# Four graph layers on one core: where TensorE's in-order list holds the probabilities-times-values step

## The reference, cut to what matters

```python
x = _layernorm(x + _L0_gnn_ref(x, adj, adj, L0_gnn_b), axis=-1)
x = _layernorm(x + _L1_gnn_ref(x, L1_gnn_W, L1_gnn_a, L1_gnn_beta, adj), axis=-1)
x = _layernorm(x + _L2_gnn_ref(x, adj, L2_gnn_weight, L2_gnn_bias), axis=-1)
x = _layernorm(x + _L3_gnn_ref(x, adj, L3_gnn_Wq, L3_gnn_bq, L3_gnn_Wk, L3_gnn_bk, L3_gnn_Wv, L3_gnn_bv), axis=-1)
```

## Time and profile before

| what | value |
|---|---|
| device time, median of 3 runs | 2768.54 us (2766.62 to 2768.99) |
| device time of the profiled execution | 2768.19 us |
| its span, first to last instruction | 2766.4 us |
| TensorE busy | 2696.7 us, 97% |
| VectorE, ScalarE, GpSimd busy | 69%, 53%, 54% |
| mean granted TensorE clock | 0.989 |

### The profile page before, as it was taken

One profiled execution on the slowest core, in us unless ns is written; L12 is line 12 of the kernel. 1 busy time (PEld: TensorE's weight loads), 2 busy tenths in 40 slices (PEclk: granted clock), 3 DMA queues, 4 the chain that ended last, 5 costly groups with the idle time before them and its releaser, 6 DMA issues.

```text
span 2766.4 us, 60531 instructions
## 1 busy us (share of the span) xinstructions
PE 2696.7 (97%) x19593; PEld 2383.7 (86%) x19593; DVE 1904.6 (69%) x6165; ACT 1470.6 (53%) x4360; POOL 1480.9 (54%) x1806
## 2 busy tenths in 40 slices
PE   4899999999999999999999999999999999999996
PEld 3788888888888888888888888888888888888886
DVE  7766766676676676776677767667667667667753
ACT  3355555555555555555555555555555555555544
POOL 5555555555555555555555555555555555555541
PEclk7999999999999999999999999999999999999998
DMA  3000000000000000000000000001000000000000
GB/s 123 16 20 28 27 23 27 27 23 27 27 23 27 20 30 27 19 31 27 19 27 31 20 27 31 19 27 31 20 27 30 20 27 29 21 27 27 13 16 24
DMA packets 41607, 75.19 MB, mean 27 GB/s; under 512 B 5584, under 2 KB 5712, under 8 KB 41424
## 3 DMA queue, kind: packets, MB, share of 16 engines
q1 hardware_dynamic: 41424, 73.49, 8.2%
HBM read 39.92 MB, written 33.55 MB: 27 GB/s over the span
## 4 chain that ended last, share of the span: by engine, by line
PE 96%; DVE 1%; issue 1%; ACT 1%; DMA 0%; SPq 0%; POOL 0%; ACTq 0%; POOLq 0%; DVEq 0%
PE rot L796 23%; PE rot L798 23%; PE rot L797 22%; PE score L944 5%; PE rot L904 5%; PE rot L896 5%; PE rot L853 4%; PE rot L952 3%; PE rot L926 2%; PE rot L873 2%; PE rot L877 2%; PE s_bank L861 1%; PE att_bank L932 0%; DVE x L644 0%; DVE att_e L659 0%
## 5 line engine op out<-in xcount | busy, mean ns | idle before, releaser
L360 POOL TENSOR_TENSOR x2b<-x,bias 128x512 f32<-128x512 f32 x128 | 207.6, 1621 | 495.3 <-DVE x L644 495.3
L338 POOL TENSOR_TENSOR ve<-mv,eps_col 128x1 f32<-128x1 f32 (+1 forms) x448 | 89.5, 200 | 666.5 <-ACT e L503 348.4
L796 PE MATMUL rot<-w_hi,y_hi 128*128 128x512 f32 x1024 | 426.3, 416 | 5.2 <-DVE y_lo L634 4.3
L798 PE MATMUL rot<-w_hi,y_lo 128*128 128x512 f32 x1024 | 404.2, 395 | 0.0
L797 PE MATMUL rot<-w_lo,y_hi 128*128 128x512 f32 x1024 | 402.9, 393 | 0.0
L549 ACT ACTIVATE probs<-score,sc_nmax 128x128 f32<-128x128 f32 x1024 | 358.9, 379 | 11.0 <-DVE sc_nmax L757 10.9
L634 DVE TENSOR_TENSOR y_lo<-rot,y_hi 128x512 fp32r<-128x512 f32 x128 | 88.5, 692 | 375.6 <-ACT y_hi L467 375.6
L796 PE MATMUL rot<-xt_hi,wk_hi 128*128 128x256 f32 x1024 | 299.8, 293 | 0.0
L798 PE MATMUL rot<-xt_hi,wk_lo 128*128 128x256 f32 x1024 | 290.2, 283 | 0.0
L798 PE MATMUL rot<-xt_hi,wq_lo 128*128 128x256 f32 x1024 | 289.8, 283 | 0.0
L797 PE MATMUL rot<-xt_lo,wq_hi 128*128 128x256 f32 x1024 | 289.7, 283 | 0.0
(11 more groups left out here) (117 smaller groups left out, 7736.4 us busy)
## 6 DMA issues: line engine op xcount, KB each, us to landing
x_in<-in_x SPq DMA_DIRECT2D x128, 256.0 KB, 2.6
out_x<-x SPq DMA_DIRECT2D x128, 256.0 KB, 2.2
probs<-in_L_gnn_W SPq DMA_DIRECT2D x1, 1024.0 KB, 7.9
v_sb<-in_L_gnn_weight SPq DMA_DIRECT2D x1, 1024.0 KB, 7.6
probs<-in_L_gnn_Wv SPq DMA_DIRECT2D x1, 1024.0 KB, 5.2
v_sb<-in_L_gnn_Wq SPq DMA_DIRECT2D x1, 1024.0 KB, 5.1
probs<-in_L_gnn_Wk SPq DMA_DIRECT2D x1, 1024.0 KB, 5.3
x<-in_L_gnn_a SPq DMA_DIRECT2D x1, 512.0 KB, 4.9
```

What stands on the lines that cost most here:

```text
L360: pool.tensor_tensor(x2b[:, :], x2[:, slot.buf(L_GCN, 2), :], bias2[:, :], ALU.add)\
L796: pe.matmul(outp, lh, rh, start=first, stop=False)
L798: return pe.matmul(outp, ll, rh, start=False, stop=last)
```

## The change

Only TensorE's list is reordered; no instruction is added or removed, and no wait is changed. PV (step 4) moves from behind w1 to directly in front of the scores (step 9), behind y2, edge and att. The four ot transposes (step 7) move behind the x3 transposes (step 10). The order of a slot becomes w1, y2, edge, att, PV, scores, x3, ot, w2, wv.

```diff
                     dense(rot[1], y1, "w1").then_inc(z1_mm, 1)
+                if slot.on(L_GCN):
...
+                    ins.then_inc(y2_mm, 1)
+                if slot.on(L_EDGE):
...
+                if slot.on(L_ATT):
+
+                    slot.wait(pe, att_n_done, L_ATT)
+                    slot.wait(pe, att_t_done, L_ATT, 1)
+                    pe.transpose(att_bank[:, 0:P], att_n[:, slot.buf(L_ATT, 2), :], ident[:, :])\
+                      .then_inc(att_t_mm, 1)
                 if slot.on(L_PV):
 
                     slot.wait(pe, pt0_done, L_PV)
...
                     ins.then_inc(pv_mm, 1)
-                if slot.on(L_GCN):
...
-                if slot.on(L_EDGE):
...
-                if slot.on(L_PV):
-
-                    slot.wait(pe, o_t_done, L_PV)
-                    for n in range(GROUP * CHUNKS):
-                        ins = pe.transpose(rot[3][:, n * P:(n + 1) * P], o_t[:, n * P:(n + 1) * P], ident[:, :])
-                    ins.then_inc(ot_mm, 1)
-                if slot.on(L_ATT):
...
                     ins.then_inc(xt_mm, 1)
+                if slot.on(L_PV):
+
+                    slot.wait(pe, o_t_done, L_PV)
+                    for n in range(GROUP * CHUNKS):
+                        ins = pe.transpose(rot[3][:, n * P:(n + 1) * P], o_t[:, n * P:(n + 1) * P], ident[:, :])
+                    ins.then_inc(ot_mm, 1)
                 if slot.on(L_GCN):
 
                     slot.wait(pe, y2_lo_done, L_GCN)
```

More of the change, by code:

```diff
@@ L933, in emit @@
                       .then_inc(att_t_mm, 1)
+                if slot.on(L_PV):
+                    slot.wait(pe, pt0_done, L_PV)
+                    slot.wait(pe, pt1_done, L_PV)
+                    if slot.part(L_PV) == 0:
+                        slot.wait(pe, v_done, L_PV - (GROUP - 1))
+                    first = slot.buf(L_PV, BUFS) // GROUP * GROUP
+                    for g in range(GROUP):
+                        for c in range(CHUNKS):
+                            at = (g * CHUNKS + c) * P
+                            for h, rows in enumerate(HEAD_ROWS):
+                                col = (slot.part(L_PV) * CHUNKS + c) * P + h * HEAD
+                                ins = pe.matmul(rot[3][rows, at:at + P], v_sb[:, first + g, col:col + HEAD],
+                                                probs_t[:, c, g * 2 + h, :], start=True, stop=True)
+                    ins.then_inc(pv_mm, 1)
                 if slot.on(L_QK):
```

## The result

The changed kernel takes 2795.58 us (median of 4 runs, 2795.36 to 2797.81) against 2767.58 us before (4 runs): a ratio of 1.0103, with a 95% interval of 1.0085 to 1.012. It is slower by 28 us. The profiled execution took 2795.51 us, its span is 2793.7 us. The forecast was 2795.6, in a range of 2778 to 2813.

What follows compares the result with a forecast made beforehand. TensorE's list, busy 97%, was taken as the bound. From 2768.19 us, 124 slots at +0.24 us (+29.8) less 2.4 us in the last slots gave +27.4, so 2795.6 us, range 2778 to 2813.

Steps and rivals of the forecast that it cites:

- The stall: TensorE at x3: y2_lo, queued on VectorE behind the o_t copy, comes late, so x3 waits 0.47 us a slot.
- PV's start: TensorE from w1 through y2, edge and att: PV would start at 1404.96, with w1's last start at 1402.94.
- x3 and ot: Eight TensorE transposes ahead of w2: 0.38 us for x3's four behind a stall, 0.44 for ot's four.
- A slot: One TensorE period, PV to PV: 20.88 us before, 0.24 us longer after, so 21.12 us.
- The signs: Expected in the profile: x3 waits about 124 times, VectorE waits some 1.5 us for PV, y2's weight-load row gone.
- How PV passes to the scores: TensorE's gap from column shape to row shape: between none (0.20 us less) and a full exit, covered by x3's stall.
- The slots 128 to 130: Last slots where PV, y2 and x3 still meet: counted at +0.24 us each, within slots 7 to 130.
- The slots 131 to 133: Three last slots with scores but no y2: ot's wait for its copy goes, giving back 3 x 0.79 = 2.4 us.
- Only the change of shape counts: Rival: VectorE's chain is not late, each slot is 0.20 us shorter, 2741 us; chance 0.07.
- The two cancel: Rival: x3's stall is real but saved bubbles offset it within 0.04 us a slot, near 2768 us; chance 0.05.
- the delay goes round: Rival: VectorE's 0.7 us delay reaches TensorE in the next slot, period grows 0.7 us, 2855 us; chance 0.04.
- rival 1: The rival "Only the change of shape counts": each slot 0.20 us shorter, 2741 us; chance 0.07.

Runs made afterwards that it cites:

- the cured kernels: Changed kernel with y2_lo ahead of the o_t copy on VectorE (2741.39 us), or with ot in front of x3 on TensorE (2739.9 us).
- three kernels: Changed kernel with y2_lo ahead of the o_t copy (2741.39 us); with ot before x3 (2739.9); with both edits plus y2_hi ahead of ScalarE's output steps (2740.44).
- both cures: Changed kernel with y2_lo ahead of the o_t copy on VectorE and ot in front of x3 on TensorE: 2751.97 us, ratio 0.9949.

## Why the prediction was right, point by point

- **The stall.** Predicted: PV's first start to the copy 1.14 us, 0.61 to `y2_lo`, 0.83 to x3, together 2.58. Measured: 1420.13 - 1418.99 = 1.14, 0.61, 1421.56 - 1420.74 = 0.82, together 2.57. x3 late by 0.47 predicted, 0.46 measured (1.55 - 1.09). Three hand-overs from other corners of the trace, where the same engines waited in the same order, carried over to 0.01 us.
- **PV's start.** Predicted 2.02 us behind the last start of w1 (1402.94 to 1404.96); measured 1418.99 - 1416.97 = 2.02. Single terms: w1 to y2 0.23 us predicted and 0.22 measured, y2 0.81 (0.81), edge 0.78 (0.79), att 0.20 (0.20).
- **x3 and ot.** Predicted 0.38 + 0.44 = 0.82 us from x3 to w2, measured 1422.38 - 1421.56 = 0.82. The two terms were each off, and only their sum fits: x3 takes 0.47 and ot 0.35.
- **A slot.** Predicted 20.88 + 0.24 = 21.12, measured 21.13; the growth is 0.25 us.
- **The signs.** The row of y2's weight load is gone, and VectorE waits 1.42 us for PV, where some 1.5 were named.
- **How PV passes to the scores.** It was left open, between nothing and a full gap. Measured is a full one: 1.02 us from PV to the scores, as 1.02 from PV to y2 before. Column shape to row shape costs what column shape to whole array does. In the changed kernel it is covered, as said; in the cured kernels it is part of the 20.68, which was worked out with the full gap.
- **The ends of the run: mis-sized, and the total close by luck.** To set both traces side by side I take the start of the probability transposes (L873), which stand in the same place in both lists. In slot 7, the first that has them, they start at 125.86 us before and 124.49 after; from there to slot 128 each slot is 0.25 us longer, 30.6 in all; over the slots 128 to 133 the difference shrinks by 1.9; together 27.3. The prediction had 0 for the slots ahead of 7, +29.0 for these 121 slots and -1.7 for the rest. Its misses of 1.6, 1.4 and 0.2 us cancel.
  - *The start.* Up to slot 7 TensorE's two lists are the same, so the 1.4 us are no effect of the change. The stretches at the lower clock fell elsewhere. From 93 to 98 us the granted clock was 0.66 before and 1.00 after, in the last column but two (columns as in the earlier trace rows), and from 80 to 92 us it was 0.86 and 0.57:

```profile
93.00:98.00 5.00, 4.79 (x16) 3.97 (x17) 4.01 (x8) 1.88 (x3) 4.92 (x4) 0.66 0.22 52
93.00:98.00 5.00, 4.81 (x23) 4.07 (x24) 4.01 (x8) 1.94 (x3) 4.92 (x4) 1.00 0.14 52
```

  - *The slots 128 to 130.* Counted at +0.24 each, they measure +0.1, +0.1 and -0.64. In slot 130 w1 has run out, and before the change PV waited 1.12 us there for `probs_t`; after it, y2 stands in front of PV and fills that wait.
  - *The slots 131 to 133.* The prediction gave back 3 x 0.79 us, since ot finds its copy ready, and it does: the row for that wait is down from four times to one, in the last slot, as said. But wv's wait for `o_norm` was looked at only where w2 stands between ot and wv. In the slots 131 and 132 there is no w2, and wv now waits 0.9 us each time (the `o_norm` row of the waits above), so they are 0.1 us longer each. Slot 133 is 1.65 us shorter, which was not foreseen either: its scores no longer stand behind ot and its wait. They start 1.02 us behind PV and not 2.93 (before, ot waited 0.78 us there and then took 1.05 us to the scores, at a granted clock of 0.57 from 2742 to 2746 us), and VectorE's first score maximum 3.42 us behind PV and not 5.06.
- **The rivals.** "Only the change of shape counts" gives 2741 us and is what happens as soon as the stall is gone: 2741.4, 2739.9 and 2740.4 us in three kernels. It was the right price for a case that VectorE's order excludes. "The two cancel" and "the delay goes round" did not occur; `o_norm` is 0.7 us later (5.69 us behind w1's last start, and not 4.99), and the idle time at the head of VectorE's slot shrank from 2.44 to 1.98 us without reaching TensorE. Of the chances, the outcomes give faster 0.08 where rival 1 has 0.07; nothing hangs on that hundredth.

The gain that one may look for in this change was there all along, 25 to 26 us of it against the kernel before in the same runs; it was lost to a new wait worth twice as much, 124 x 0.46 = 57 us.

## What to carry to other kernels

Where two engines work through fixed lists and hand work to each other twice (PV to copy to ot, y2 to y2_lo to x3), look at who waits at the head of the other list. When a step is moved late on one engine, everything queued on the other behind the instruction that waits for it becomes late too; either move the step that is needed soonest ahead of that instruction, or put the freed work in front of the step that will be late. Equal order of the pairs in both lists is no rule by itself. In the changed kernel VectorE delivers the copy first and TensorE asks for `y2_lo` first, and that costs 0.46 us a slot; with ot late and PV early the orders differ too and cost some 4 us at most, as the copy is long done; with both cures they differ, and that costs 12 us, or nothing once `y2_hi` comes early. Differing orders cost what the operand is late, so the distances have to be added up each time.

A bound engine with 97% busy still gives something through order alone: here one change of array shape a slot, 1% of the time.

## What I had not expected

Two sound cures were worse together than either alone (2752 against 2741 and 2740 us), since each rests on another order of the same two VectorE steps. And a wait of TensorE can be real without a row in the view of its matmuls: 0.15 us in every other slot, some 10 us in all, showed there only as a distance of starts (1.25 against 1.10 us). The view of its weight load named it at once, so it belongs beside the other whenever two slots of one loop differ.
